# Step sizes of a state-space scan: a Softplus pass on ScalarE in place of relu, exp, ln and a VectorE maximum

## The reference, cut to what matters

```python
x_in, z = split(x @ Wi.T + bi)                      # 512 channels each
u  = silu(causal_conv4(x_in) + conv_b)
dt = softplus(x_in[..., :32] @ Wdt.T + bdt)         # the step sizes, one per token and channel
# for every channel and each of its 16 states:
h  = h * exp(dt * A) + dt * Bm * u                  # A = -exp(A_log)
y  = sum over the states of h * Cm
out = (y * silu(z)) @ Wo.T + bo + x * mean(Dv)
```

## Time and profile before

| what | us |
|---|---|
| median of three runs | 760.28 |
| the profiled execution, as a whole | 761.95 |
| its span, first to last instruction | 760.1 |
| VectorE (DVE) busy | 666.6 |
| TensorE matmul (PE) busy | 644.2 |
| ScalarE (ACT) busy | 607.4 |
| GpSimd (POOL) busy | 293.8 |
| mean granted TensorE clock, share of full speed | 0.926 |

### The profile page before, as it was taken

One profiled execution on the slowest core, in us unless ns is written; L12 is line 12 of the kernel. 1 busy time (PEld: TensorE's weight loads), 2 busy tenths in 40 slices (PEclk: granted clock), 3 DMA queues, 4 the chain that ended last, 5 costly groups with the idle time before them and its releaser, 6 DMA issues. The chain is left out here.

```text
span 760.1 us, 8303 instructions
## 1 busy us (share of the span) xinstructions
PE 644.2 (85%) x2928; PEld 333.1 (44%) x2928; DVE 666.6 (88%) x450; ACT 607.4 (80%) x1074; POOL 293.8 (39%) x184
## 2 busy tenths in 40 slices
PE   7867786799896999979798999994977997798857
PEld 5632333364342466445144575531231553265435
DVE  2437947879999999999999999999999999999971
ACT  2488896879889989998788989898888787866663
POOL 0107020134344588479912565046970060600010
PEclk9997998989997899999899999997997999899879
DMA  8431465341838070431658070614234331605001
GB/s 294 148 138 43 164 225 164 133 172 32 320 104 315 7 245 5 160 117 49 227 150 301 34 236 0 231 47 166 84 146 132 139 111 71 206 28 221 1 1 55
DMA packets 40026, 103.08 MB, mean 136 GB/s; under 512 B 4080, under 2 KB 13040, under 8 KB 39984
## 3 DMA queue, kind: packets, MB, share of 16 engines
q1 hardware_dynamic: 37424, 94.40, 34.2%
q10 hardware_dynamic: 2560, 8.14, 4.6%
HBM read 23.08 MB, written 4.19 MB: 36 GB/s over the span
## 5 line engine op out<-in xcount | busy, mean ns | idle before, releaser
L1124 ACT ACTIVATE G<-RD,COL 128x1024 f32<-128x1024 f32 (+1 forms) x288 | 280.0, 1042 | 56.2 <-PE Y L1424 50.8
L1246 DVE TENSOR_TENSOR_SCAN G<-G,STT,RV 128x1024 f32<-128x1024 f32 (+1 forms) x160 | 312.5, 2016 | 1.5 <-ACT G L1124 1.5
L1246 DVE TENSOR_TENSOR_SCAN G<-G,RV 128x1024 f32<-128x1024 f32 (+1 forms) x128 | 268.7, 2155 | 13.9 <-ACT G L1124 13.8
L1424 PE MATMUL Y<-G,RW 128*32 128x512 f32 x1024 | 144.6, 682 | 49.4 <-DVE G L1246 46.1
L849 POOL TENSOR_SCALAR LV<-LV 128x4 f32<-128x4 f32 x18 | 17.3, 962 | 226.4 <-ACT XN L944 226.1
L858 POOL TENSOR_TENSOR LV<-LV,HALF 128x4 f32<-128x4 f32 (+1 forms) x25 | 47.8, 1913 | 135.8 <-DVE LV L1201 134.3
L1424 PEld LDWEIGHTS Y<-G,RW 128*32 128x32 f32 x1024 | 28.0, 117 | 127.6 <-DVE G L1246 64.6
L875 POOL TENSOR_SCALAR XN<-X,LV 128x256 f32<-128x256 f32 x36 | 75.9, 2113 | 1.9
L1391 PE MATMUL MB<-XI,DIAG 128*64 128x512 f32 x248 | 64.3, 656 | 12.7 <-DMA XI<-XI 10.8
L1350 PE MATMUL MB<-MT,XF 128*128 128x256 f32 x240 | 59.6, 393 | 9.9 <-ACT MT L986 7.6
L1369 PE MATMUL MB<-XT,WI 128*128 128x512 f32 x128 | 63.4, 624 | 3.7 <-ACT XT L970 3.7
(11 more groups left out here) (96 smaller groups left out, 779.7 us busy)
## 6 DMA issues: line engine op xcount, KB each, us to landing
RD<-DW SPq DMA_DIRECT2D x60, 512.0 KB, 3.7
RV<-DW SPq DMA_DIRECT2D x60, 512.0 KB, 4.9
W<-in_w SPq DMA_DIRECT2D x48, 256.5 KB, 3.6
XI<-XI ACTq DMA_DIRECT2D x30, 256.5 KB, 5.6
X<-in_x SPq DMA_DIRECT2D x8, 512.0 KB, 6.3
out<-X SPq DMA_DIRECT2D x7, 512.0 KB, 3.3
G<-in_w SPq DMA_DIRECT2D x4, 513.0 KB, 8.4
RV<-in_w SPq DMA_DIRECT2D x4, 513.0 KB, 12.3
```

The lines of the kernel that those rows point to most:

```text
L1124: eng.activation(G[:, i % NG, t0:t1], RD[:, q, t0:t1], ACT.Exp, scale=NAC[:, states(i):states(i) + 1]).then_inc(sems["exp"])
L1246: eng.tensor_tensor_scan(g, g, RV[:, (4 * k + q) % NR, t0:t1], STT[:, idx:idx + 1] if goes_on else 0.0, ALU.mult, ALU.add).then_inc(sems[" ...
L1424: ins = eng.matmul(Y[32 * q:32 * q + 32, 512 * h:512 * h + 512], RW[:, states(i + o), :], G[:, (i + o) % NG, 512 * h:512 * h + 512], start ...
```

## The change

Softplus becomes one ScalarE instruction that reads PSUM and writes `DW`: over 1024 tokens where the two banks are adjacent, else twice over 512. The stages `dtr`, `dte`, `dtl`, `topc` and the constants `TOPC` and `HIGH` go. Stage `dt` moves from VectorE to ScalarE. In `dts` a table load `softset` stands ahead of it and a load `unset`, back to the set of exp and ln, behind it; all three are issued in one step, with no slots of rest. In `half` (block 0) there is `softset` and no `unset`, because the Silu load follows; `dt` and its `repd` of both halves now come ahead of Silu.

```diff
@@ LOAD
-        "z": (0, 30), "dtr": (0, 25), "dte": (0, 48), "dtl": (0, 48), "silu": (0, 57), "expset": (0, 57),
+        "z": (0, 30), "softset": (0, 57), "dt": (0, 62), "silu": (0, 57), "expset": (0, 57), "unset": (0, 57),
@@ def dts(k)
         for hf in range(2):
             do("dm", k, hf)
         yield 0
-        for hf in range(2):
-            do("dtr", k, hf)
-        do("dte", k, 0)
-        yield 0
-        do("dtl", k, 0)
-        yield from rest_for(REST)
+        do("softset", k, 0)
         do("dt", k, 0)
+        do("unset", k, 0)
@@ def half(k, hf)
         do("dm", k, hf)
-        do("dtr", k, hf)
-        do("dte", k, hf)
-        do("dtl", k, hf)
         yield 1
         do("um", k, hf)
+        do("softset", k, hf)
+        do("dt", k, hf)
+        for q in range(4):
+            do("repd", k, q, hf)
         if hf == 0:
-            do("dt", k, hf)
-            for q in range(4):
-                do("repd", k, q, hf)
             yield 0
         do("silu", k, hf)
         do("u", k, hf)
         do("expset", k, hf)
-        if hf:
-            for _ in range(HREST[0]):
-                yield 0
-            do("dt", k, hf)
-            for q in range(4):
-                do("repd", k, q, hf)
-        for _ in range(HREST[2] if hf else 1):
+        for _ in range(HREST[0] + HREST[2] if hf else 1):
             yield 0
         do("w", k, hf)
@@ ScalarE
-                elif stage == "dtr":
...
-                    eng.activation(DW[:, 0, 512 * hf:512 * hf + 512], bank("dm", k, hf), ACT.Relu, scale=-1.0,
-                                   bias=TOPC[:, k % 4:k % 4 + 1]).then_inc(sems["dtr"])
-                elif stage == "dte":
...
-                    eng.activation(d, d, ACT.Exp, scale=-1.0, bias=HIGH[:, 0:1]).then_inc(sems["dte"])
-                elif stage == "dtl":
...
-                    eng.activation(d, d, ACT.Ln, bias=1.0).then_inc(sems["dtl"])
-                elif stage == "expset":
+                elif stage == "softset":
+                    eng.preload_act_table_set("softplus")
+                elif stage == "dt":
+                    k, p = a
+                    for hf in halves(k, p):
+                        e.wait_ge("dm", k, hf)
                     if k:
                         e.wait_ge("w", *before(k))
                         for r in replicated(k - 1):
                             if r[0] == "repd":
                                 e.wait_ge(*r)
+                    first = count.bank["dm", (k, halves(k, p)[0])]
+                    wide = len(halves(k, p)) == 2 and count.bank["dm", (k, 1)] == first + 1
+                    for hf in [halves(k, p)] if wide else [[h] for h in halves(k, p)]:
+                        o = MB[:, first:first + 2, :].rearrange("p a n -> p (a n)") if wide else bank("dm", k, hf[0])
+                        ins = eng.activation(DW[:, 0, 512 * hf[0]:512 * hf[-1] + 512], o, ACT.Softplus,
+                                             bias=COL[:, BDT + k % 4:BDT + k % 4 + 1])
+                    ins.then_inc(sems["dt"])
+                elif stage in ("expset", "unset"):
                     eng.preload_act_table_set("natural_log_exp_and_others")
@@ VectorE
-                elif stage == "topc":
...
-                elif stage == "dt":
...
-                        ins = eng.scalar_tensor_tensor(out=d, in0=o, scalar=COL[:, BDT + k % 4:BDT + k % 4 + 1], in1=d,
-                                                       op0=ALU.add, op1=ALU.max)
-                    ins.then_inc(sems["dt"])
```

More of the change, by code:

```diff
@@ L14 @@
 EPS = 1e-5
-TOP = 17.0
 AL, BB, CC, BI, CWT, CB, BDT, B2, DV, ID, CW0, BX, NCOL = 0, 64, 128, 192, 200, 216, 220, 224, 240, 244, 372, 376, 377
@@ L533, in schedule @@
         do("wa", n)
-    for stage in ("ones", "half", "calm", "warm", "b2q", "topc", "nae"):
+    for stage in ("ones", "half", "calm", "warm", "b2q", "nae"):
         do(stage)
@@ L680, in build @@
         HALF = sb("HALF", [P, 4])
-        HIGH = sb("HIGH", [P, 1])
         ZERO = sb("ZERO", [P, 3])
-        TOPC = sb("TOPC", [P, 4])
         RW = sb("RW", [P, 64, 32])
@@ L841, in do @@
                 elif stage == "half":
-                    eng.memset(HIGH[:, :], TOP)
                     eng.memset(ZERO[:, :], 0.0)
@@ L1077, in do @@
                                    bias=COL[:, BI + 4 + k % 4:BI + 5 + k % 4]).then_inc(sems["z"])
-                elif stage == "dtr":
-                    k, hf = a
-                    e.wait_ge("dm", k, hf)
-                    e.wait_ge("topc")
+                elif stage == "softset":
[4 more added lines that the diff above has]
+                        e.wait_ge("dm", k, hf)
                     if k:
@@ L1162, in do @@
                     eng.tensor_scalar(DM[:, 1:2], DM[:, 2:3], 1.0 / 512 / 256, None, ALU.mult).then_inc(sems["dmu"])
-                elif stage == "topc":
-                    e.wait_ge("col")
-                    eng.tensor_scalar(TOPC[:, :], COL[:, BDT:BDT + 4], -1.0, TOP, ALU.mult, ALU.add).then_inc(sems["topc"])
                 elif stage == "b2q":
```

## The result

The changed kernel took 782.98 us (median of 4 runs, 782.45 to 786.57) against 761.19 us for the one before; the ratio is 1.029, with a 95% interval of 1.0237 to 1.0344. The forecast of 750 us, faster, was wrong, and the time lies outside its range.

A forecast was written before the change was run, and what follows sets the result against it. VectorE (DVE) was taken to set the pace in the steady stretch. Its saving of 15.4 us, less 4.8 lost and 0.8 for ScalarE, plus 1 gained in the filling, gave -10.8 us: 750 us, range 741 to 767.

The forecast's parts named there:

- Waits and queues: Semaphore waits, DMA issue, PSUM release and the re-drawn plan, in which other chains slip by a slot: 0, 3 us both ways.
- one wait of 1.49 us: VectorE's wait for an exp behind a table load, ending at 352.80 us; a slip could add or spare it twice.
- Its own sign of being wrong: Prediction wrong if Softplus exceeds 2 us, VectorE's idle grows over 8 us, or the plan moves a chain onto the path.
- VectorE's part: Steady stretch: 14 maximum instructions leave VectorE's queue, taking 15.4 us off the path.
- four blocks' worth: Two stretches where neighbours are as full as VectorE: 4.8 us of its saving lost, bounds 0 and 9.6 us.
- block 11: Example of uneven slack: first exp done about 1.1 us after 591.60, its scan starts at 599.30, a margin of 6.6 us.
- ScalarE's part: Per block, two loads and Softplus add 3.75 us against 3.5 removed: 0.2 us more, 2.6 us over 13 blocks.
- where ACT has slack this costs nothing: ScalarE's extra work counts only in the four blocks of the two full stretches, 0.8 us.
- The banks: Two PSUM banks come free some five slots (11 us) sooner; nobody waits for that release, so by itself nothing.
- The sum: -15.4 + 4.8 + 0.8 - 1 = -10.8 us: the profiled execution becomes 751.2, the median 749.5, said as 750 us.
- Case C: ScalarE's queue between two groups of exps: dear Softplus, from about 2.4 us more a block, starves scans; 768 us, chance 0.14.
- Case B: VectorE's saving swallowed: 9.6 us lost, no gain in the filling, 3 us of bad plan; 758.5 us, chance 0.26.

The follow-up runs named there:

- experiment 11: The changed kernel with all nine forced steps at their old slots and the excursion priced at 98 units instead of 176: 750.88 us, ratio 0.9873.
- experiment 10: The changed kernel with all nine forced steps at their old slots (seven at unit 27, two at unit 41), price 176 kept: 761.40 us, ratio 1.0011.
- experiment 9: The changed kernel with two extra forced steps of all chains at unit 41: 767.26 us, ratio 1.0089.
- experiment 6: The kernel before with only VectorE's maximum left out; relu, exp and ln kept, same plan: 756.26 us, ratio 0.993.
- experiment 1: The kernel before's plan, stage for stage, with the change's operations (Softplus and its table loads, no maximum): 756.83 us, ratio 0.995.
- experiment 7: The kernel before's plan with one Relu pass per block in place of Softplus and no table loads around it: 745.02 us, ratio 0.9787.

## Why the prediction was wrong

**The step that failed** is the last sentence under "Waits and queues": the re-drawn plan, put "at 0" with "3 us both ways". It is worth 32 us: 783.0 against 750.9 in experiment 11, where only the plan differs. The prediction had named both things that move the plan (176 units for 98 and 48, and the banks that come free five slots sooner). It took the second for nothing, and priced the first from one wait of 1.49 us. That the early `dt` takes forced steps away from every other chain it did not see. Its own sign of being wrong, VectorE's idle time up by more than 8 us, came: 38.7. The row of that wait shows a plan that fits; it does not show what a slip adds when it puts the copy that TensorE waits for behind exps and an excursion. The split; the rows on forced steps rest on one pair each:

| part of the plan | pairs | us |
|---|---|---|
| price of 176 units | 783.0 to 775.1; 766.8 to 756.5; 761.4 to 750.9 | 8 to 10.5 |
| forced steps that no longer occur at units 27 and 41 | 783.0 to 761.4 (experiment 10) | 21.6 |
| of these the two at unit 41 | 783.0 to 767.3 (experiment 9) | 15.7 |
| `dt` early, with nine stages around block 2 | 766.8 to 761.4; 756.5 to 750.9 | -5.4 to -5.6 |

**VectorE's part.** The 15.4 us left its queue. That four blocks' worth would not reach the end was too little: experiment 6 shows that 10.3 of 15.4 us are lost in the old plan, just past the bound of 9.6 that the text kept. Where they go was not followed block by block. (Block 0 has 32 units, so the rows at 582 to 603 us that the text calls block 11 are block 12; their margin of 6.6 us stands.)

**ScalarE's part** was right for the operations. Softplus took 1.115 us. In the timeline of experiment 11 a load and what follows are 1.29 us apart, and 169.01 + 1.28 = 170.29 is followed by the next instruction at 170.30. The Trainium skill's page ScalarE: Activation LUTs (What ACT_TABLE_LOAD costs) has 2.66 us for a switch; no run here shows the drain that would make up the difference. But "where ACT has slack this costs nothing" was too simple: the switches cost 11.8 us in the old plan (experiments 1 and 7), and the kernel is no slower for it only because the removed relu, exp and ln had cost about as much (experiments 1 and 6, 756.8 and 756.3 us).

**The banks.** "By itself nothing" was wrong with the other sign: an early `dt` is worth about 5.5 us in two pairs of runs. Whether by the banks, by the product `w` of block 2 or by its Silu, which stand one and two slots sooner with it, was not separated.

**The sum.** With nearly the old order of the other chains the forecast's 749.5 us met 750.9. That is in part luck, two errors that cancel: VectorE's saving taken too high and the early `dt` left at nothing.

**The rivals.** Case C (Softplus and loads too dear) had the right sign, but its mechanism fell: its place was to be ScalarE's queue between two groups of exps, and its condition, 2.4 us more a block, is not met. Case B's "bad plan" was held at 3 us. The right rival would have been the plan itself, read off before the forecast: the list of slots of the kernel before shows which `until` force steps, and that `w` of block 2, one of them, depends on the slot of `dt`.

## What to carry to other kernels

Where one program orders the work of all engines, a change of price, place or release time of one stage re-draws the order for all, and in in-order queues that can cost more than the operations changed (32 us lost here, against some 9 gained in experiment 11). Make such a change in two steps: first swap the operations inside the old order, then move the order, and look at each. And look for side effects that the plan lives on by accident: here a stage that was late forced steps for all chains, and curing the lateness moved them. A stall can cost twice: here TensorE's granted clock was 0.56 behind its wait, and it ran matmuls that the others waited for at that pace.

## What the runs showed of the hardware that was not expected

Relu, exp and ln over 1024 elements with their maximum left out, and Softplus with two table loads, cost the same within 3 us over 17 excursions in either plan: a table load of 1283 ns showed up in ScalarE's queue as one more short instruction, with the next one 1.29 us after its start. Softplus from two adjacent PSUM banks (1115 ns for 1024) took about as long as a ln from SBUF (1057 ns) or an exp with a bias (1149 ns). Behind waits of 3.22 and 6.28 us TensorE's granted clock was 0.52 and 0.56, and eight matmuls took 3.62 us that took 1.89 us a little later.
